# Attention across the batch: the last two queries halved once by VectorE, their four blocks summed by TensorE behind the logits

## The reference

```python
x = ...                       # (8, 512, 256): S = 8, B = 512, H = 256
ln1 = _layer_norm(hidden_states, ln1_weight, ln1_bias)
qkv = einsum('sbh,oh->sbo', ln1, qkv_weight)   # 16 query heads of 16, 4 groups of keys and values
scores = einsum('bgqsd,bgtd->bgqst', q, k) * scale
scores = where(tril, scores, min)              # query s sees keys 0..s
ao = einsum('bgqst,bgtd->bgqsd', softmax(scores), v)
h1 = hidden_states + ao @ proj_weight.T
ln2 = _layer_norm(h1, ...)                     # then router logits and a mixture of 8 experts, top 2
```

## Time and profile before

| | us |
|---|---|
| median of 3 runs | 3178.55 |
| lowest, highest | 3178.43, 3184.07 |
| the profiled execution | 3178.36 |
| its span | 3176.6 |

### The profile page before, as it was taken

The page is one execution under the profiler, slowest core; times in us unless marked ns, Lnnn a source line. Parts: engine busy times, 40 slices in busy tenths (PEclk is TensorE's granted clock), DMA queues, the critical chain, the costliest instruction groups (busy, mean ns, idle before and its releaser), DMA issues. The chain is left out here.

```text
span 3176.6 us, 53101 instructions
## 1 busy us (share of the span) xinstructions
PE 2883.2 (91%) x20844; PEld 1985.0 (62%) x20844; DVE 1658.0 (52%) x5041; ACT 1369.4 (43%) x3001; POOL 853.0 (27%) x828
## 2 busy tenths in 40 slices
PE   7889999876999999999999999999999688679992
PEld 3566666653666666666757576656666456478882
DVE  4677766735555544444444544445554488531114
ACT  3666666623445353544444444444443221112222
POOL 1001111123323333223232322333333100025554
PEclk9999999987999999999999999999999899669996
DMA  4111011004000000000000000000000000113325
GB/s 138 18 23 20 18 18 21 5 2 163 8 4 9 6 31 14 1 1 1 16 29 1 1 1 13 28 5 11 6 11 6 10 13 15 66 30 79 75 84 179
DMA packets 66232, 93.96 MB, mean 30 GB/s; under 512 B 9971, under 2 KB 52982, under 8 KB 64944
## 3 DMA queue, kind: packets, MB, share of 16 engines
q1 hardware_dynamic: 58304, 74.24, 8.0%
q0 software_dynamic: 7680, 16.32, 2.0%
HBM read 59.31 MB, written 27.36 MB: 27 GB/s over the span
## 5 line engine op out<-in xcount | busy, mean ns | idle before, releaser
L1336 PE MATMUL bank<-h2T,w 128*128 128x512 f32 x1024 | 479.4, 606 | 5.1 <-ACT gT L1274 3.7
L1374 PE MATMUL bank<-w,gT 128*128 128x256 f32 x2048 | 465.9, 381 | 0.0
L1374 PEld LDWEIGHTS bank<-w,gT 128*128 128x128 f32 x2048 | 379.3, 190 | 49.7 <-issue 0.5
L1011 POOL TENSOR_TENSOR prob<-prob,rsum 128x512 f32<-128x512 f32 (+1 forms) x256 | 237.8, 949 | 590.3 <-DVE rsum L1158 590.3
L1336 PEld LDWEIGHTS bank<-h2T,w 128*128 128x128 f32 x1024 | 182.4, 190 | 224.1 <-issue 173.9
L1274 ACT ACTIVATE gT<-bank,vec 128x512 f32<-128x512 f32 x256 | 175.1, 687 | 286.1 <-PE bank L1336 284.6
L576 ACT ACTIVATE y<-y,least 128x128 f32<-128x128 f32 (+3 forms) x512 | 252.0, 554 | 50.5 <-DVE least L456 50.5
L456 DVE CUSTOM_DVE_ANT_0 y<-bank,mask 128x128 f32<-128x128 f32 (+3 forms) x512 | 223.9, 485 | 70.1 <-PE bank L673 68.7
L1164 DVE COPY probT<-bank 128x1024 f32<-128x1024 f32 (+1 forms) x128 | 139.2, 1087 | 227.4 <-PE bank L1390 227.4
L1135 DVE CUSTOM_DVE_ANT_0 prob<-bank,mask 128x256 f32<-128x256 f32 (+1 forms) x512 | 164.2, 386 | 167.3 <-PE bank L1326 167.3
L1246 ACT ACTIVATE prob<-prob,least 128x256 f32<-128x256 f32 (+1 forms) x512 | 239.5, 469 | 15.8 <-DVE least L1135 15.5
(11 more groups left out here) (297 smaller groups left out, 4991.1 us busy)
## 6 DMA issues: line engine op xcount, KB each, us to landing
w<-in_W SPq DMA_DIRECT2D x8, 1024.0 KB, 5.3
expert_parts<-zeros SPq DMA_DIRECT2D x8, 1024.0 KB, 15.7
we<-in_we SPq DMA_DIRECT2D x16, 512.0 KB, 5.3
rows<-modulation SPq DMA_DIRECT2D x40, 128.0 KB, 2.9
x<-in_x SPq DMA_DIRECT2D x8, 512.0 KB, 6.4
prob<-score SPq DMA_DIRECT2D x64, 64.0 KB, 2.4
probT<-score SPq DMA_DIRECT2D x64, 64.0 KB, 2.3
token_rows<-rows_normed SPq DMA_DIRECT2D x4, 1024.0 KB, 4.4
```

The source lines that it names most:

```text
L1011: nc.gpsimd.tensor_tensor(two, two, rsum[:, at:at + 2].unsqueeze(2).to_broadcast([P, 2, width]), ALU.mult).then_inc(s["probs"], 1)
L1336: ins = nc.tensor.matmul(M[m % 2][:, :], w1[:, k, m * P:(m + 1) * P], h2T[:, k, :], start=(k == 0), stop=(k == KD - 1))
L1374: ins = nc.tensor.matmul(M[i][:, (t % 2) * D:(t % 2 + 1) * D], gT[:, m, t * P:(t + 1) * P], w2[:, m, :], start=(m == 0), stop=(m == MF - 1))
```

## The change

Queries 6 and 7 are halved once by VectorE: of the three levels of `reduced` only the first stays, and leaves four blocks of each in `pairs`. TensorE sums these with the identity, as it does for the others: a new piece AV 3, 2 x 4 matmuls, and a copy by ScalarE. AV 3 stands last in `gaps[9]`, behind AV 2 and, from tile 1 on, behind the logits LG; it waits for `reduced`. All four PROJ now wait for their AV to be copied. The products of the next tile come in the order 2, 3, 0, 1, 4, 5, 6, 7, and those of query 6 wait until AV 3 has been summed. Since one piece more stands in each tile, the two misc banks change places for some of what follows.

```diff
+HALVED = 4
@@ gaps_of
-    gaps[9] = [("AV", j, p) for j in (1, 0)] + turned + [("AV", 2, p)] + logits
+    gaps[9] = [("AV", j, p) for j in (1, 0)] + turned + [("AV", 2, p)] + logits + [("AV", 3, p)]
@@ products
-                for i in (2, 3, 0, 1, 6, 7, 4, 5):
-                    if p and ch == 0 and i in (0, 2, 4):
+                for i in (2, 3, 0, 1, 4, 5, 6, 7):
+                    if p and ch == 0 and i % 2 == 0:
                         full(dve, ("AV", i // 2, p - 1))
-                    if p and ch == 0 and i == 6:
-                        dve.wait_ge(s["reduced"], p)
@@ reduced
                 nc.vector.tensor_tensor(last[0][:, :, 0:3, :], last[0][:, :, 0:3, :], last[0][:, :, 4:7, :], ALU.add)
-                steps(nc.vector.tensor_tensor(last[1][:, :, 0:4, :], last[1][:, :, 0:4, :], last[1][:, :, 4:8, :],
-                                              ALU.add))
-                for one in last:
-                    ins = nc.vector.tensor_tensor(one[:, :, 0:2, :], one[:, :, 0:2, :], one[:, :, 2:4, :], ALU.add)
-                steps(ins)
-                for par, one in enumerate(last):
-                    ins = nc.vector.tensor_tensor(aoT[:, :, 6 + par, :], one[:, :, 0, :], one[:, :, 1, :], ALU.add)
-                ins.then_inc(s["reduced"], 1)
+                nc.vector.tensor_tensor(last[1][:, :, 0:4, :], last[1][:, :, 0:4, :], last[1][:, :, 4:8, :],
+                                        ALU.add).then_inc(s["reduced"], 1)
@@ work, on TensorE
                     if kind == "AV":
-                        pe.wait_ge(s["weighted"], len(EXPANDS) * p + WHOLE[i])
+                        if i == 3:
+                            pe.wait_ge(s["reduced"], p + 1)
+                        else:
+                            pe.wait_ge(s["weighted"], len(EXPANDS) * p + WHOLE[i])
                         out = bank.rearrange("p (c a n) -> p c a n", c=2, n=P)
                         for a in range(2):
                             q = 2 * i + a
-                            for t in range(q + 1):
+                            blocks = HALVED if i == 3 else q + 1
+                            for t in range(blocks):
                                 ins = nc.tensor.matmul(out[:, :, a, :], c.ident[:, :],
                                                        pairs[:, pair_of(q)[0], :, offset_of(q) + t, :],
-                                                       start=(t == 0), stop=(t == q))
+                                                       start=(t == 0), stop=(t == blocks - 1))
                     if kind == "PROJ":
-                        if i < 3:
-                            drained(pe, ("AV", i, p))
-                        else:
-                            pe.wait_ge(s["reduced"], p + 1)
+                        drained(pe, ("AV", i, p))
```

## The result

| | before | changed |
|---|---|---|
| median of 13 runs, us | 3182.78 | 3189.40 |
| lowest to highest | 3178.08 to 3187.93 | 3186.64 to 3194.43 |
| ratio, 95% interval | | 1.0023 [1.0015, 1.0032] |
| profiled execution, its span | 3178.36, 3176.6 | 3189.40, 3187.7 |

The changed kernel is 7.3 us slower by the ratio (4.8 to 10.2; the medians as they stand differ by 6.6), against +9.55 forecast. The prediction counted from a median of 3178.55 us and so said 3188.0; the thirteen runs of the kernel before have a median of 3182.78. The execution profiled before was one of the faster ones of its kernel, the one after lies on its median, so the two spans differ by more, 11.1 us.

What follows compares the result with a forecast made beforehand. VectorE was taken to bound tile 0, TensorE tiles 1 and 2, with VectorE only waiting for projections in tile 3; -0.95 + 3 x 3.5 = +9.55 us gave 3188.0 us (+0.30%), range 3184.0 to 3191.5.

Steps and rivals of the forecast that it cites:

- Its own sign of being wrong: Tile 1: wrong if VectorE's addition reading PROJ 1's bank starts less than 2 us later behind AV2, or tile 3's projections no later.
- Tile 0, -0.95 forecast: Tile 0, bound by VectorE: of 2.0 us of additions removed only 0.95 won, as the normalisation then waits for GpSimd's rstd.
- the price of rstd: Tile 0, GpSimd: 0.63 us of rstd's work done beside the large addition, 1.04 us undisturbed after, ending at 2570.1 (bounds 2569.80, 2570.61).
- the 1.3 us left out: Tile 0: the filled TensorE gap would restore the clock over the scores, 1.3 us, left out because VectorE ends last.
- Tile 1, +3.5 forecast: Tile 1: TensorE has no slack behind LG, so AV3 moves PROJ 1 and VectorE's addition back by its whole 3.5 us.
- Tile 2, +3.5 forecast: Tile 2: TensorE bound as in tile 1, VectorE waiting 1.04 us for PROJ 1, so all of AV3's 3.5 us shows.
- third fall: Rival: TensorE's clock falls in tile 2 too, 1.7 us more, +11.25 in all, 3189.7 us; chance 0.24.
- Tile 3, +3.5 forecast: Tile 3: AV3 lies between LG and four projections that VectorE only waits for, so all 3.5 us show.
- The price of a fall there: Tile 3's projections: a fall of TensorE's clock costs 8.61 - 2 x 3.70 = 1.2 us.
- The bound of -2.9 us for both falls: Tiles 1 and 3: 2.9 us less if neither clock fall behind LG happens.
- The low end of the range, 3184.0: Whole kernel: the forecast less both clock falls and the larger bound of tile 0's gain, 3184.0 us.
- The hidden pieces: Query 6's wait for AV3 hidden by 0.7 us, ScalarE's 0.58 us copy hidden; VectorE's waits grow 5.5 us in tiles 1 and 2.

Runs made afterwards that it cites:

- adds_kept: Changed kernel with VectorE's four small additions done as before but into scratch, AV3 kept on TensorE; ratio 1.0027 against the kernel before.
- adds_gone: Kernel before with VectorE's four small additions left out and nothing given to TensorE; ratio 0.9997 against the kernel before.
- reduced_first: Changed kernel with both large VectorE additions ahead of the statistics for tile p + 2; one run, 3189.45 us.
- tile0_only: Changed kernel with AV3 in tile 0 alone, VectorE summing queries 6 and 7 as before in tiles 1 to 3; ratio 0.9997 against the kernel before.
- before_router_last: Kernel before with tile 3's router turns and logits (of tile 2) moved behind PROJ 3; ratio 0.9965 against the kernel before.
- big_in_two: Changed kernel with VectorE's addition of 1024 elements done as two of 512; one run, 3194.52 us.
- combined_mid: AV3 in tile 0 only, normalisation between queries 5 and 6, tile 3's router work last, LG of tiles 1 and 2 behind PROJ 1; ratio 1.0002 against the kernel before.

## Why the prediction was right, and where it was off

*Direction and size.* Forecast +9.55 us (+0.30%), measured +7.3 (4.8 to 10.2). The mechanism was the one named: AV3's 3.5 us on TensorE's path in tiles 1 to 3, little from VectorE. `adds_kept` and `adds_gone` show both halves apart. That 3189.40 us lies inside the stated range is partly luck: the prediction counted from 3178.55, and from the later median of the kernel before, 3182.78, the same +9.55 would have given 3192.3, above the range. A difference 2.3 us smaller than forecast and a base 4.2 us higher offset each other.

*Its own sign of being wrong.* The prediction called itself wrong if added 1 of tile 1 started less than 2 us later behind AV2. It starts 13.77 us behind AV2 before (2633.87 - 2620.10) and 15.53 after (2635.68 - 2620.15), 1.76 us later, so by the two profiles that sign appeared. What it caught is the clock, which fell in that stretch before and not after. With a fall on both sides the delay is 3.44 us (`reduced_first`, 2638.12 - 2620.91 = 17.21), without one on either side 2.87 (`tile0_only`, about 12.66). The row of the first, VectorE in tile 1 of `reduced_first`:

```profile
2638.12 0.69 DVE L1790 TENSOR_TENSOR y<-y,bank 128x512 f32<-128x512 f32 x1 [0.63 <-PE bank L1919]
```

The sign was written without fixing the clock. Tile 3's projections do start later (23.09 us behind AV1 instead of 17.86).

*Tile 0, -0.95 forecast, -0.57 measured.* The order of the waits was right: `reduced` gone, rstd late next. The step that failed is the price of rstd, where 0.63 of 1.67 us of work was reckoned as done beside the addition, at a reduced pace. The wait for the running addition was added whole instead, so rstd ended 2.48 us after its start, at the far bound that the prediction gave, and the normalisation started 0.46 us earlier behind AV1 (8.56 us instead of 9.02), not 0.95. The other 0.11 us is a second misreading: the last two additions of tile 0 took 1.46 us where the same pair takes 1.28, so VectorE already waited 0.2 us there for PROJ 3 (which ended at 2586.33; the addition began at 2586.37), and the low clock behind the idle time was not off the path. Filling the gap gives that back; of the 1.3 us left out it is 0.1 here, 0.33 once VectorE is earlier (`adds_gone`), more where the low clock lasts longer (`before_router_last`).

*Tile 1, +3.5 forecast.* Like against like it is 2.87 us without a fall of the clock (55.88 and 53.01) and 3.46 with one on both sides (57.57 in `reduced_first`, one run of a kernel that also differs in VectorE's order, and 54.11 before). The wait of 1.01 us for PROJ 1, from which the prediction read "bound by PE", was there only because a fall of 1.7 us lay over the projections in that execution. At full clock VectorE is later by about 0.6 us. The term was mis-sized by that much; the measured +1.77 is 3.46 less 1.69 for the fall that the profiled execution of the changed kernel did not have there.

*Tile 2, +3.5 forecast.* 3.44 without falls (54.76 in `reduced_first`, 51.32 before), 3.47 with one on both sides. Here "bound by PE" holds at full clock: VectorE waited 3.61 and 1.04 us before. The +5.14 of the two profiles is this and a fall that came instead of tile 1's: the rival "third fall" had the place right, but the fall moved rather than being added.

*Tile 3, +3.5 forecast.* 3.65 and 3.69 measured; in the second, 0.2 is a low clock at the start of AV1 that lasted a little longer (6.65 us against 6.43). The price of a fall there, 8.61 - 2 x 3.70 = 1.2 us, was reckoned too low: the four projections take 7.07 us in one piece at full clock (`before_router_last`), so the fall cost 1.5 us in them and 0.2 in LG (3.86 instead of 3.63). The bound of -2.9 us for both falls should have been -3.4. The low end of the range, 3184.0, does not come out of the terms named for it either: they give 3184.8.

*The hidden pieces.* The wait of query 6's products for AV3 is as computed (added 0 done, then 0.63 us of waiting for PROJ 1, 0.7 computed). The copy by ScalarE and PROJ 3's new wait cost nothing that shows. VectorE's waits between `reduced` and added 1 grew by 3.7 us in tile 1 (1.56 for rstd, 2.53, 0.63, less the 1.01 of before), not by 5.5, and by 7.3 us in tile 2; both differences are again the fall. With it on both sides tile 1 gives 5.4 us, and with its 1.69 us taken out tile 2 gives 5.6.

*The sum.* With equal clocks the stages give -0.6 + 2.9 to 3.5 + 3.5 + 3.6 = +9.4 to +10.0 us, in the upper half of what the timing allows (4.8 to 10.2), so the median difference of 7.3 needs no further cause. The low clock in tile 0, which only kernels with the gap there pay, may have a part in it; how long it lasts was seen in a few executions only, and that stays open.

## What to carry to other kernels

A wait that shows one engine as the bound in one execution can be the doing of a low clock in that very stretch; take the low clock out of the row before deciding which engine is late, since the two may lie within a microsecond. Work moved from a half-used engine to the one that the others wait for cost 2.9 to 3.7 us of its 3.5 us here, and the relief of the first engine paid for at most 0.6 of it; it paid only where the second sat idle, as in tile 0. Look for work that can leave the path: two pieces of router work moved into a gap behind the last projections gave 11 us (8.3 to 14.3), more than any division of the sum tried here, but first see who empties the bank that the moved piece will take. And when you write down what would show a forecast wrong, say at which clock it is to be read.

## What the runs showed of the hardware

GpSimd's `tensor_tensor` on eight elements a partition lasted 2.48 us when a VectorE addition of 1024 elements with two SBUF inputs was running at its start, 1.95 behind one of 512, 1.67 with none. The extra time is what that addition had left, less about 0.1 us; the next addition added nothing. Nor did GpSimd's work lengthen VectorE's: in the kernel before, the two additions of 512 elements took 1.29 us in tile 0, with GpSimd computing rstd beside them, and 1.29 us in tile 2, with GpSimd idle. A long VectorE addition can so delay a tiny GpSimd instruction: by 0.81 us of its 1.22 here. Where the GpSimd result is awaited, a shorter VectorE instruction ahead of it helped (VectorE's wait fell from 1.57 to 0.97 us, tile 0 from 49.98 to 49.44).

In each of the thirteen profiled executions TensorE's granted clock was low at or behind the 16 matmuls of 8 columns in tile 1 or tile 2: in exactly one of the two in eleven (f in the tables), in both in two, `big_in_two` and `combined_mid`. In `combined_mid` TensorE had sat idle ahead of them (4.35 and 1.07 us); in the others no idle time between the end of AV0 and the fall was longer than 0.2 us. What decides between the two tiles no run shows. A fall cost 1.7 us where only the matmuls behind LG ran slow (5.39 us for 3.70) and 3.4 where the end of LG did too (4.35 and 6.33 for 3.63 and 3.70).
